# A first stage with loads four ahead and wider stores, and experts that read result rows ahead of weight pieces

## The reference

```
x = x + L0_xattn(layernorm(x), ctx, ctx, ...)   # 16 heads of 16; keys in a window of 64; q and k turned (rope)
x = x + L0_ffn(layernorm(x), ...)               # a gated recurrence over the batches
x = x + L1_xattn(layernorm(x), ctx, ctx, mask)  # full attention over 1601 keys
x = x + L1_ffn(layernorm(x), ...)               # 8 experts, top 2, capacity 2150, hidden 1024, exact gelu
```

## Time and profile before

| | us |
|---|---|
| median of 3 runs | 5928.07 |
| lowest, highest | 5923.93, 5930.05 |
| the profiled execution | 5923.17 |
| its span | 5921.4 |

### The profile page before, as it was taken

The page is one execution under the profiler, slowest core; times in us unless marked ns, Lnnn a source line. Parts: engine busy times, 40 slices in busy tenths (PEclk is TensorE's granted clock), DMA queues, the critical chain, the costliest instruction groups (busy, mean ns, idle before and its releaser), DMA issues. The chain is left out here.

```text
span 5921.4 us, 92268 instructions
## 1 busy us (share of the span) xinstructions
PE 4985.4 (84%) x28783; PEld 2858.6 (48%) x28784; DVE 3911.4 (66%) x7722; ACT 2693.4 (45%) x3563; POOL 949.6 (16%) x754
## 2 busy tenths in 40 slices
PE   5787997998679999999999999999977039999970
PEld 3444664776234444444444444444335037777750
DVE  4555665663548888887888788888736136666653
ACT  1223553222327777766767667767621013433320
POOL 3440001221510000000000000000012520000016
PEclk8988998998779999999999999999877569999985
DMA  6445664222753334343333333333134331211125
GB/s 221 119 120 149 164 166 130 84 80 81 209 120 60 50 60 69 68 70 56 60 70 70 69 68 59 51 61 57 30 107 138 117 99 57 70 57 51 60 70 183
DMA packets 344094, 544.33 MB, mean 92 GB/s; under 512 B 54880, under 2 KB 256063, under 8 KB 341488
## 3 DMA queue, kind: packets, MB, share of 16 engines
q1 hardware_dynamic: 325648, 487.83, 34.8%
q0 software_dynamic: 14768, 50.51, 2.5%
q10 hardware_dynamic: 3264, 0.79, 0.1%
HBM read 271.54 MB, written 187.80 MB: 78 GB/s over the span
## 5 line engine op out<-in xcount | busy, mean ns | idle before, releaser
L1180 DVE TENSOR_REDUCE full_peak<-full_item 128x1 f32<-128x512 f32 (+2 forms) x3392 | 2036.0, 655 | 466.9 <-PE full_item L1247 461.5
L1150 ACT ACTIVATE full_prob<-full_score 128x1024 f32<-128x1024 f32 (+1 forms) x1792 | 1650.2, 960 | 647.4 <-PE full_score L1258 641.3
L1247 PE MATMUL full_item<-full_kst,full_qst 49*128 49x512 f32 (+1 forms) x4096 | 1203.9, 406 | 44.4 <-DVE full_peak L1180 24.1
L1258 PE MATMUL full_score<-full_qst,full_kst 51*128 51x512 f32 (+1 forms) x3328 | 1110.3, 448 | 17.4 <-ACT full_prob L1150 12.1
L1258 PEld LDWEIGHTS full_score<-full_qst,full_kst 51*128 51x128 f32 (+1 forms) x3328 | 480.4, 183 | 932.2 <-ACT full_prob L1150 602.4
L1272 PE MATMUL full_value<-full_prob,full_vaug 128*17 128x512 f32 x6656 | 887.8, 606 | 0.8 <-ACT full_raw L1137 0.7
L1247 PEld LDWEIGHTS full_item<-full_kst,full_qst 49*128 49x128 f32 x4096 | 631.3, 189 | 189.2 <-DVE full_peak L1180 129.3
L2620 PE MATMUL moe_ybank<-moe_w_both,moe_h_high 128*128 128x512 f32 x1088 | 414.7, 420 | 54.2 <-DVE moe_y L2568 54.2
L2517 ACT ACTIVATE moe_h<-moe_hbank,moe_b 128x512 f32<-128x512 f32 (+1 forms) x320 | 199.5, 624 | 548.8 <-PE moe_hbank L2610 541.8
L754 DVE TENSOR_REDUCE win_peak<-win_item 128x2 f32<-128x384 f32 x512 | 262.7, 553 | 126.2 <-PE win_item L794 119.1
L728 ACT ACTIVATE win_prob<-win_score 128x768 f32<-128x768 f32 x256 | 207.4, 811 | 276.1 <-PE win_score L808 272.8
(11 more groups left out here) (275 smaller groups left out, 7149.7 us busy)
## 6 DMA issues: line engine op xcount, KB each, us to landing
full_kst<-full_high SPq DMA_DIRECT2D x256, 200.1 KB
full_ctxT<-in_ctxT SPq DMA_DIRECT2D x16, 1601.0 KB
full_kst<-full_low SPq DMA_DIRECT2D x128, 200.1 KB
win_qst<-scratch_q SPq DMA_DIRECT2D x384, 64.0 KB
full_qst<-scratch_q SPq DMA_DIRECT2D x384, 64.0 KB
scratch_xbuf<-ctxp_zero POOLq DMA_DIRECT2D x17, 1024.0 KB
scratch_attn<-win_raw SPq DMA_DIRECT2D x64, 256.0 KB, 2.1
scratch_q<-open_parts SPq DMA_DIRECT2D x64, 256.0 KB, 3.5
```

Source lines behind the costliest of these rows:

```text
L1150: nc.scalar.activation(prob[h][(s.par * PAIRS + t) % 2][0:rows, 0:banks, :], score[u % 2][0:rows, 0:banks, :], ACT.Exp, scale=SCALE).then_ ...
L1180: nc.vector.tensor_reduce(peak[s.par][:, hq:hq + len(qts), c], src, AX, ALU.max).then_inc(item_read, 1)
L1247: ins = nc.tensor.matmul(ps[:, at:at + z - a], qst[s.slot][rows, h // 2, qt * P:(qt + 1) * P].bitcast(F32R), kst[s.slot][rows, h // 2, a:z ...
L1258: ins = nc.tensor.matmul(score[u % 2][0:z - a, kt % 2, :], kst[s.slot][rows, h // 2, a:z].bitcast(F32R), qst[s.slot][rows, h // 2, :].bitc ...
```

## The change

In project_context:

- x and ctxT have four buffers each. The loads of batches 0 to 3 are issued at the start (0 ahead of the constants, 1 behind them, 2 and 3 behind the mask), those of batch n + 4 in pass n, behind the q stores of pass n - 1.
- The transposes have two banks of their own; the ten other jobs of a pass go round six banks. The transposes of pass n + 1 stand on TensorE between W1 and R2a of pass n. xn, xnT and the parts have two buffers each.
- DVE measures (statistics) and centres two passes ahead, and takes the rests of units 2 and 3 right after turn 0, the rest of 0 after turn 1.
- A unit's three parts leave in one transfer for each of its two groups of 64 partitions, thus two transfers in place of six; each moves 192 rows of 1 KB (the three parts lie 64 KB apart in DRAM).
- The 17 zeroing transfers are spread over the passes, one in each and two in the last.
- All 16 passes are written out; there is no Fori in the stage. Each unit has its own semaphores.

In experts, `read_rows` of a chunk's tiles comes first, and the weight pieces are spread between them: pieces follow tiles 1, 2 and 3 in chunks 1 and 2 (one each), tiles 1 and 3 in chunk 3.

```diff
-    ring = Ring(jobs, 8)
+    JOBS = ["R0a", "R0b", "R1a", "R1b", "W0", "W1", "R2a", "R2b", "R3a", "R3b"]
+    RING = 6
+    BUFS = 4
+        tbank = [s.ps(f"tbank{i}", [P, 512]) for i in range(KC)]
+        parts = [[s.sb(f"parts{i}{u}", [P, PART, SQ], BF16) for u in range(UNITS)] for i in range(2)]
...
             def store_parts(n, u):
-                for part in range(PART):
-                    for gg in range(2):
-                        sp.dma_start(rows[g + gg, 64 * part:64 * part + 64],
-                                     parts[u][64 * gg:64 * gg + 64, part, :]).then_inc(parts_out[u], 16)
+                for gg in range(2):
+                    sp.dma_start(rows[g + gg].rearrange("(t m) k -> m t k", t=PART),
+                                 parts[n % 2][u][64 * gg:64 * gg + 64, :, :]).then_inc(parts_out[n % 2][u], 16)
+            for n in range(BATCH):
+                if n > 0:
+                    store_parts(n - 1, 2)
+                    store_parts(n - 1, 3)
+                if n + BUFS < BATCH:
+                    loads(n + BUFS)
+                sp.wait_ge(read, job("W1", n) + 1)
+                sp.dma_start(d["v0"][n].rearrange("(i p) f -> p i f", p=P), v0[n % 2][:, :, :]).then_inc(v0_out[n % 2], 16)
                 store_parts(n, 0)
                 store_parts(n, 1)
...
         def _(pool):
+            for n in range(BATCH):
                 add(n, 0)
+                if n > 0:
+                    low(n - 1, 2)
                 add(n, 1)
+                if n > 0:
+                    low(n - 1, 3)
+                if n + 2 < BATCH:
+                    power(n + 2)
                 low(n, 0)
                 low(n, 1)
+                for k in range(n * ZEROS // BATCH, (n + 1) * ZEROS // BATCH):
+                    zero_rows(k)
                 add(n, 2)
                 add(n, 3)
...
         def _(act):
+            read_turned(0)
+            for n in range(BATCH):
+                high(n, 0)
+                if n > 0:
+                    mid(n - 1, 2)
+                high(n, 1)
+                if n > 0:
+                    mid(n - 1, 3)
                 mid(n, 0)
+                if n + 1 < BATCH:
+                    read_turned(n + 1)
                 mid(n, 1)
                 high(n, 2)
                 high(n, 3)
...
         def _(dve):
+            for n in range(BATCH):
                 turn(n, 0)
+                if n > 0:
+                    rest_of(n - 1, 2)
+                    rest_of(n - 1, 3)
+                if n + 2 < BATCH:
+                    measure(n + 2)
                 turn(n, 1)
                 rest_of(n, 0)
+                values(n)
+                if n + 2 < BATCH:
+                    centre(n + 2)
                 rest_of(n, 1)
...
                 turn(n, 2)
                 turn(n, 3)
...
         def _(pe):
+                if n + 1 < BATCH:
+                    transposes(n + 1)
+                pe.wait_ge(t_read, KC * n + KC)
                 for u in (2, 3):
-                    turned_pair(n, u, xnT)
+                    turned_pair(n, u, xnT[n % 2])
...
 def experts(nc, d):
-                    if not last:
-                        for j in PIECES_IN.get(c, ()):
-                            split_weights(n + 1, 1 - par, j)
                     at_least(dve, y_out[parity(par, c)], before(n, par, c))
+                    pieces = () if last else PIECES_IN.get(c, ())
                     for i in range(z - a):
                         read_rows(n, par, c, i)
+                        for j in pieces[i * len(pieces) // (z - a):(i + 1) * len(pieces) // (z - a)]:
+                            split_weights(n + 1, 1 - par, j)
```

More of the change, by code:

```diff
@@ L300, in power, with zero_rows, add, low @@
                 nc.gpsimd.tensor_tensor(rstd[:, :], var_eps[:, :], minus_half[:, :], ALU.pow).then_inc(rstd_done, 1)
+            def zero_rows(k):
+                rows = d["xbuf"].rearrange("(p r) f -> p (r f)", p=P)
+                pool.dma_start(rows[:, k * 2048:(k + 1) * 2048], zero[:, :]).then_inc(xbuf_zeroed, 16)
+            def add(n, u):
+                pool.wait_ge(read, job(f"R{u}b", n) + 1)
+                if n > 0:
+                    pool.wait_ge(rest_done[u], n)
+                nc.gpsimd.tensor_tensor(whole[u][:, :], turned[u][:, :], other[u][:, :], ALU.add).then_inc(whole_done[u], 1)
+            def low(n, u):
+                pool.wait_ge(mid_done[u], n + 1)
+                nc.gpsimd.tensor_tensor(parts[n % 2][u][:, 2, :], rest[u][:, :], parts[n % 2][u][:, 1, :],
+                                        ALU.subtract).then_inc(low_done[u], 1)
             power(0)
@@ L420, in _, with values @@
-            normalise(0, 0)
-            scale_rows(0, 0)
+                        out=to[u][:, :], in0=bank[j % RING][:, :], scalar=b[bias_of][:, c:c + 1],
+                        in1=table[:, :], op0=ALU.add, op1=ALU.mult).then_inc(read, 1)
+            def values(n):
+                if n >= 2:
+                    dve.wait_ge(v0_out[n % 2], 16 * (n // 2))
+                for t in range(2):
+                    j = job(f"W{t}", n)
+                    dve.wait_ge(full, j + 1)
+                    nc.vector.tensor_tensor(v0[n % 2][:, 2 * t:2 * t + 2, :],
+                                            bank[j % RING][:, :].rearrange("p (i f) -> p i f", i=2), bv0[:, :, :],
+                                            ALU.add).then_inc(read, 1)
```

258 lines of the change are left out of this document (96 added, 162 removed).

## The result

| | before | after |
|---|---|---|
| median of 4 runs, us | 5927.84 | 5708.26 |
| lowest, highest | 5923.93, 5930.05 | 5702.82, 5711.07 |
| the profiled execution | 5923.17 | 5711.07 |
| its span | 5921.4 | 5709.0 |

The ratio is 0.9628, with a 95% interval from 0.9613 to 0.9643: 3.7% faster. The prediction was 5719, with a range of 5690 to 5775.

The account below looks back on a forecast made before the run. The circle through SyncE's queue bounded the first stage, and VectorE's moe_y work held up the experts. 5923.2 less 133 (first stage) and 75 (experts) gives 5715, plus 4.9 for the median 5719 us; range 5690 to 5775.

Parts of the forecast that it names:

- The circle through SyncE's queue: First stage before: next x load waits behind 24 q and k stores, which wait for compute on x; 26.27 us a pass.
- The store's issue, 0.65 with bounds of 0.39 and 1.95: First stage, SyncE: issuing one new 192-row store was taken as 0.65 us, between 0.39 and 1.95.
- The rival in which transfers bind: First stage: stores of 2.6 us each make SyncE need 22.1 us a pass; kernel 5762 us, chance 0.15.
- the slower case: First stage: stores beyond 3.9 us each make the kernel slower than before, 6005 us at 4.5 each; chance 0.02.
- The ring, 19.4 taken between 18.1 and 19.9: First stage: hand-overs VectorE, GpSimd, ScalarE sum to 19.9 us a pass, TensorE's work to 18.1; 19.4 taken.
- The meetings: First stage: VectorE and GpSimd operations that overlap slow each other, about 2.7 us of the ring's 19.9 a pass.
- The stage's sum, 335.5 at its end: First stage: start, fourteen passes at 19.4, last two passes and tail end it at 335.5 us against 468.8, 133 less.
- TensorE's floor, 18.1 to 18.2: First stage: TensorE's own work without pauses takes 18.1 to 18.2 us a pass.
- The rival that it binds: First stage: TensorE binds because meetings cost little; pass 18.15 us, kernel 5700 us, chance 0.27.
- The zeros, some 25 us: First stage before: 17 zeroing transfers of 1 MB issued together cost about one further pass, some 25 us.
- Experts: fourteen chunks at 23.2, 75 us: Experts: chunks 1 and 2 of seven experts fall from 400.2 us together to 325, 75 less.
- Everything else unchanged: Stages outside project_context and the experts: predicted difference 0 us, full attention included.

Follow-up runs that it names:

- experiment 5: Kernel before with only one part of the change, two store transfers a unit in place of six: 5815.0 us, first stage 369.2 us.
- Experiment 4: Kernel after with six store transfers a unit again, everything else as after the change: 5726.09 us, ratio 0.9667.
- experiment 3: Kernel after with GpSimd's reciprocal root (power) for pass n + 2 moved ahead of the second add of pass n: 5696.8 us, ratio 0.9623.
- experiment 7: Kernel after with all 17 zeroing transfers issued together in the first pass: 5704.77 us, first stage 328.5 us.
- experiment 8: Kernel after with the experts' weight pieces behind all readings of a chunk's result rows, not between them: 5714.06 us, experts 859.6 us.
- experiment 10: Kernel before plus 130 already satisfied waits (65 instructions) at the start of TensorE's first stage: 5932.94 us, full attention 2687.2 us.
- experiment 9: Kernel of experiment 3 plus 382 already satisfied waits (191 instructions) at the start of TensorE's first stage: 5696.13 us, ratio 0.9616.

## Why the prediction came out

**The circle through SyncE's queue.** Right, and shown by experiment 5: shortening the queue alone ends it. The prediction counted the loads ahead, the doubled buffers and the banks as parts of one step; the runs show that they overlap with the short queue instead of adding to it: 99 us by the one, 127 by the others, 145 by all. Experiment 4 adds that with these others in place even a queue longer than the pass doesn't hold the passes up in this stage.

**The store's issue, 0.65 with bounds of 0.39 and 1.95.** A median of 0.60 to 0.69 for the issue itself, 0.70 to 0.76 by the measure of the earlier trace rows. The value of the nearest shape held. The rival in which transfers bind and the slower case needed 2.6 and 3.9 us.

**The ring, 19.4 taken between 18.1 and 19.9.** Right as to what binds (the root ends VectorE's longest wait, and TensorE is next, as experiment 3 shows), 0.83 us too long. One sign of the prediction so failed: steady loads 19 to 20 us apart; they came every 18.57. The terms between one third add and the next, on the timeline above, were predicted 19.9 and measured 18.57. The statistics to the next turn took 1.85, not 2.19; centring 2.2, not 2.5; the root 1.07 with its hand-over, not 1.25; add, add and rests 3.64, not 3.75; the reads of unit 1, 1.49, not 1.6; lows, mids and casts with their hand-overs make up the remaining 0.3.

The meetings were real and came nearly at their full price: add1 with rest0 beside it took exactly the 1.65 of the earlier trace rows; the rests of units 2 and 3 had to let the next add pass, as the sum had it; centring took 2.22 where experiment 3, which moves it beside other work, has 1.38. So what was too dear was less the meetings than the ordinary terms, and taking 19.4 for a sum of 19.9 was a step in the right direction for the wrong reason. Of the Trainium skill's rule of an exclusive lock, "SBUF — State Buffer", section "SBUF: two separate sides", the trace thus agrees in kind: a rest that began inside an add took 2.30 us where it takes 0.68 alone. It stood behind the next add as well, which is more than the one instruction of the rule.

**The stage's sum, 335.5 at its end, 323.4 measured.** Its terms missed in both directions. Counted at the ends of VectorE's reads of the first pair: the first one at 22.8 us, not 21.7; then fourteen passes in 258.4, not 271.6 and 1.8 for the mask (of these 15.0 less 11.6 are the shorter pass, the rest three early passes of 18.06 and a mask that cost nothing); the fifteenth 15.9, not 17.5; the last 13.75, not 14.5. That makes 16.3 us less. The tail took 12.6, not 8.4, and gave 4.2 back: in the last pass two zeroing transfers of 1 MB stand beside the last stores, and single issues took up to 2.5 us there. In experiments 5 and 7, which have no zeros at the end, the tail is 10.4 and 10.6.

**TensorE's floor, 18.1 to 18.2.** Measured 18.06 in experiment 3; three passes of experiment 7 at 17.8 to 17.9 with TensorE busy throughout show that even this isn't the least. The rival that it binds was 0.5 us away, and one moved operation made it true. The measured time, 5708, lies as near to this rival's 5700 as to the forecast's 5719.

**The zeros, some 25 us.** Right for the kernel before, of which it was said: between VectorE's first reads of a pass, the two passes of the burst take 42.95 and 36.95 us there, against 26.3 of a steady one, 27 us more. The prediction counted the burst as gone and put one issue of 0.56 us into the ring of each pass against it, and so much experiment 7 shows it to cost there (18.57 less 18.06). It didn't ask what the spreading is worth net: 6.6 us without the lead of loads and 5.9 with it (369.2 to 362.6 and 328.5 to 322.7).

**Experts: fourteen chunks at 23.2, 75 us.** The chunks 1 and 2 fell from 400.2 to 324.2 us, 76.0 less, as reckoned from the earlier trace rows. The step that failed was to leave chunk 3 out of the sum: it fell from 23.5 to 22.5 us in all seven, 7.0 less. The earlier trace rows had the hint, three waits an expert, of which the third was chunk 3's. The rest, 1.1, is scattered over the first chunks. The fifth chunk was named as one that may be 1 us late. It wasn't late at all with the pieces spread (9.24 us before and after), and experiment 8 shows that this was the right place to worry: with them last it is 1.1 to 3.8 late.

**Everything else unchanged.** This failed: full attention lost 13.4 us, 12.8 of them in the two pauses at TensorE's jumps (18.0 less 5.2). That the change writes out sixteen passes was in the diff, and no step of the prediction asked what more code ahead does to a later loop; the term was put at nothing without a reason. By luck it masked the two gains that were reckoned too small: 208 us were predicted for the profiled execution, 212.1 came.

## What to carry to other kernels

When a DMA queue's issues lie on the critical circle, look first whether several transfers can be one: here a transfer with three times the rows took at most 0.14 us more to issue, and this one edit alone made two thirds of the stage's gain. A queue that is longer than a pass may leave the passes as they are while buffers last, and then show at the end of the stage: compare the pass and the tail, not only the stage. Spreading transfers that nobody waits for trades one burst for a price in every pass; reckon both. Put work that is only preparation in the gaps behind what frees a bank, in pieces no longer than the gap. After a large change compare stages that it doesn't touch, too: code that grows ahead of a loop can move the loop to a place where it has to wait for one more instruction fetch at its jump.

## What the runs showed of the hardware

TensorE's pause at a jump back of a loop was 2.3 to 3.0 us or 8.0 to 9.5, in the same code, according to where the loop lies in the program (places 0 and 192 against 65 of 256 instructions, 16 KB); in experiment 10 it came in two pieces of up to 4.9, 6.8 to 7.5 together. The fetches themselves are much the same in all kernels: a second piece of 16 KB follows the first by 5.7 to 7.3 us, and TensorE goes on 2.4 to 3.2 us after the start of a fetch. What differs is whether it goes on after the first (the short pause), only after the second (the long one), or, in experiment 10, for 0.7 and 1.2 us after the first and then again after the second. That the second comes so late because the batch's load is under way fits the window of the pause, in which the DMA engines are busy 0.71 of the time, against 0.52 just ahead of it:

```profile
2566.00:2571.60 5.60, 5.23 (x37) 1.69 (x35) 5.40 (x10) 3.81 (x6) 0.00 (x0) 1.00 0.52 66
2571.60:2581.47 9.87, 0.41 (x4) 0.01 (x1) 0.67 (x2) 0.00 (x0) 0.00 (x0) 0.61 0.71 255
```

That part is argued, not shown: no run moved the load. It can't be that the fetch waits for the whole load, for in experiment 3 it starts at 2572.1 and the load lands at 2575.2. Between kernels at the same place, full attention still differed by up to 13 us (2686.6 in experiment 3, 2700.0 in experiment 4), and that stays open.

An already satisfied wait cost TensorE 0.054 us, 0.108 for the instruction that holds two (experiment 9). A transfer of 192 rows of 1 KB took SyncE a median of 0.60 to 0.69 us to issue, one of 64 rows 0.47 in the loop of the kernel before and 0.60 in written-out passes (its last two, and experiment 4), one of 512 rows 0.39 in the kernel before and 0.55 in the kernel after. A VectorE operation on two tensors in SBUF that begins inside a GpSimd add took 2.30 us in place of 0.68 and ended only behind the next add, too.
